# Who issues the expert weights: from ScalarE's queue to SyncE's, at fixed steps

## The reference, cut to what matters

```python
x = x + ss2d(group_norm(x))        # conv 3x3, then a scan over 2304 tokens with 16 states per channel
t = t + linear_attention(ln(t))
t = t + moe(ln(t))                 # the part that the change is about

def moe(x, Wg, W1, W2, W3, b3):    # 8 experts, F = 384, two experts a token
    top_logits, top_idx = top_k(x @ Wg, 2)
    C = sum(onehot(top_idx) * softmax(top_logits)[..., None], axis=-2)
    h = einsum('bsd,edf->bsef', x, W1)
    g = einsum('bsd,edf->bsef', x, W3) + b3
    return einsum('bse,bsef,efd->bsd', C, silu(h) * g, W2)
```

## Time and profile before

| | |
|---|---|
| median of 3 runs | 3860.7 us (3859.01 to 3863.91) |
| the profiled execution | 3844.76 us, span 3842.9 us |
| busy: PE, DVE, ACT, POOL | 3126.6, 3057.3, 2347.0, 2822.3 us |
| w_up and w_down issued by ACT | 258 each |
| w_up and w_down issued by SP | 86 each |

### The profile page before, as it was taken

How to read it: one execution, slowest core, us unless ns; L and a number is a source line. 1 busy time by engine, 2 the same in 40 slices (tenths; PEclk the granted TensorE clock), 3 DMA queues, 4 the chain that set the end, 5 groups by cost and what they waited for, 6 DMA issues and landing times.

```text
span 3842.9 us, 68512 instructions
## 1 busy us (share of the span) xinstructions
PE 3126.6 (81%) x17390; PEld 1997.4 (52%) x17390; DVE 3057.3 (80%) x5492; ACT 2347.0 (61%) x5132; POOL 2822.3 (73%) x2969
## 2 busy tenths in 40 slices
PE   5687888778889888898889888898889888777772
PEld 3233344335556555664556555564556555557772
DVE  2698989998898798888898788888898788944541
ACT  3354576456857766666856767576766767566331
POOL 1465667696758887788968888688968889786534
PEclk9788899789989998999989999999999999888996
DMA  3965656465769678786868768785878867875883
GB/s 85 222 148 132 150 130 171 109 164 136 217 175 258 178 189 213 214 226 155 233 181 240 190 180 223 197 247 142 234 187 237 209 169 211 222 205 186 256 261 117
DMA packets 420320, 730.00 MB, mean 190 GB/s; under 512 B 56203, under 2 KB 313814, under 8 KB 417750
## 3 DMA queue, kind: packets, MB, share of 16 engines
q1 hardware_dynamic: 327190, 534.99, 54.7%
q10 hardware_dynamic: 74304, 152.60, 12.9%
q0 software_dynamic: 18432, 37.93, 3.6%
HBM read 596.93 MB, written 100.07 MB: 181 GB/s over the span
## 4 chain that ended last, share of the span: by engine, by line
POOL 25%; issue 24%; PE 21%; DVE 16%; ACT 7%; DMA 3%; SPq 1%; ACTq 1%; POOLq 1%; DVEq 0%; PEldq 0%
POOL prod L731 12%; DVE state L1652 6%; PE ps_conv L934 5%; PE ps_main L1000 4%; DVE ps_x L1639 3%; POOL got L854 3%; POOL rows_in L831 2%; POOL hidden L843 2%; PE ps_y L1014 2%; PE ps_h L1106 2%; PE ps_x L948 1%; DMA dt_rep<-dt_dram 1%; POOL big_k L808 1%; DMA w_up<-in_w_exp 1%; PE ps_g L1149 1%
## 5 line engine op out<-in xcount | busy, mean ns | idle before, releaser
L731 POOL TENSOR_TENSOR prod<-state,c_rep 128x384 f32<-128x384 f32 x1536 | 1532.7, 1007 | 588.8 <-DVE state L1652 570.6
L1652 DVE TENSOR_TENSOR_SCAN state<-dt_rep,carry,ps_x 128x384 f32<-128x384 f32 x1280 | 1285.6, 1004 | 0.0
L1639 DVE TENSOR_TENSOR ps_x<-ps_x,db_rep 128x384 f32<-128x384 f32 x1536 | 853.1, 555 | 243.4 <-PE ps_x L948 227.9
L1265 ACT ACTIVATE dt_rep<-dt_rep,vecs 128x768 f32<-128x768 f32 x768 | 717.6, 935 | 141.2 <-DMA dt_rep<-dt_dram 101.0
L948 PE MATMUL ps_x<-x_stack,copy 96*128 96x384 bf16 x1536 | 533.8, 350 | 314.7 <-DVE state L1652 309.5
L934 PE MATMUL ps_conv<-gx,w_conv 128*128 128x384 f32 x1728 | 688.0, 505 | 7.8 <-DVE parts L1669 4.6
L948 PEld LDWEIGHTS ps_x<-x_stack,copy 96*128 96x128 bf16 x1536 | 153.8, 100 | 687.1 <-DVE state L1652 495.1
L934 PEld LDWEIGHTS ps_conv<-gx,w_conv 128*128 128x128 f32 x1728 | 300.0, 194 | 216.7 <-issue 128.7
L854 POOL DMA_INDIRECT got<-rows_out,row_of x288 | 279.8, 972 | 132.9 <-DMA rows_out<-u_out 73.0
L1014 PE MATMUL ps_y<-prod,fold 128*32 128x384 f32 x3072 | 359.6, 543 | 19.7 <-POOL prod L731 14.0
L831 POOL DMA_INDIRECT rows_in<-big_u,row_of x288 | 289.4, 1005 | 101.8 <-issue 96.2
(11 more groups left out here) (272 smaller groups left out, 5416.7 us busy)
## 6 DMA issues: line engine op xcount, KB each, us to landing
dt_rep<-dt_dram SPq DMA_DIRECT2D x384, 768.0 KB
w_up<-in_w_exp ACTq DMA_DIRECT2D x258, 384.0 KB
w_down<-in_w_exp ACTq DMA_DIRECT2D x258, 193.5 KB
w_up<-in_w_exp SPq DMA_DIRECT2D x86, 384.0 KB
x_stack<-parts SPq DMA_DIRECT2D x576, 48.0 KB
u_in<-rows_in SPq DMA_DIRECT2D x344, 64.5 KB
rows_out<-u_out SPq DMA_DIRECT2D x344, 64.0 KB
dt_dram<-dt SPq DMA_DIRECT2D x192, 96.0 KB
```

The costliest lines, as they stand in the source:

```text
L731: pool.tensor_tensor(prod[:, k % HS, :], state[:, k % HS, :], c_rep[:, c % 2, :], ALU.mult).then_inc(s_prod.sem, 1)
L1265: act.activation(dt_rep[:, g % XS, q:q + 2, :], dt_rep[:, g % XS, q:q + 2, :], ACT.Exp, scale=decay_rate).then_inc(s_decay.sem, 2)
L1639: dve.tensor_tensor(x_n, x_n, db_rep[:, c % 2, :], ALU.mult).then_inc(s_inflow.sem, 1)
L1652: dve.tensor_tensor_scan(state[:, k % HS, :], dt_rep[:, g % XS, q, :], ps_x[k % XB][:, 0:T], init, ALU.mult, ALU.add).then_inc(s_state.sem, 1)
```

## The change

For all eight images SP reads the experts' numbers and issues both transfers; ACT does neither any more. The first three tiles' weights keep their steps. Those of tile u + 3 of the images 0 to 5 are issued by SP at step TILE[u] + 5 (`T_SPW`), after a wait until ACT has read ps_g of tile u. The last two images keep TILE[u] + 2 and their wait, with one `apart()` more between the wait and the load of the number.

```diff
+T_SPW = 5
 ...
             def weights(m, u):
                 e = sp.value_load(expert_of[0:1, parity(m), u:u + 1], min_val=0, max_val=NE - 1)
                 tall = a["w_exp"][bass.ds(e, 1)].rearrange("o p f -> p (o f)")
-                sp.dma_start(w_up[:, u % WA, :], tall[:, 0:2 * F]).then_inc(s_up[u % WA].sem, 16)
-                if u >= WB:
+                if True:
+                    sp.dma_start(w_up[:, u % WA, :], tall[:, 0:2 * F]).then_inc(s_up[u % WA].sem, 16)
+                if late(m) and u >= WB:
                     due(sp, s_low, m - (B - 2), u - WB + 1)
                 sp.dma_start(w_down[:, u % WB, :], tall[:, 2 * F:3 * F + MF]).then_inc(s_down[u % WB].sem, 16)
...
                 for u in range(WA):
-                    if late(m) and t == T_W + 2 * u:
+                    if t == T_W + 2 * u:
                         if u == 0:
                             due(sp, s_sorted, m, 2)
                             apart()
                         weights(m, u)
-                u = tile_of.get(t - 2)
-                if late(m) and u is not None and u + WA < NU:
-                    sp.wait_ge(*full(m, f"g{u}"))
+                u = tile_of.get(t - (2 if late(m) else T_SPW))
+                if u is not None and u + WA < NU:
+                    sp.wait_ge(*(full if late(m) else read)(m, f"g{u}"))
+                    apart()
                     weights(m, u + WA)
...
-            def weights(m, u):
-                e = act.value_load(expert_of[0:1, parity(m), u:u + 1], min_val=0, max_val=NE - 1)
-                tall = a["w_exp"][bass.ds(e, 1)].rearrange("o p f -> p (o f)")
-                act.dma_start(w_up[:, u % WA, :], tall[:, 0:2 * F]).then_inc(s_up[u % WA].sem, 16)
-                act.dma_start(w_down[:, u % WB, :], tall[:, 2 * F:3 * F + MF]).then_inc(s_down[u % WB].sem, 16)
...
-                if u + WA < NU:
-                    weights(m, u + WA)
...
-                for u in range(WA):
-                    if t == T_W + 2 * u and not late(m):
-                        if u == 0:
-                            due(act, s_sorted, m, 2)
-                            act.sem_inc(s_sp.sem, 1)
-                        weights(m, u)
```

## The result

The changed kernel took 3886.1 us (median of 4, 3882.8 to 3891.6) against 3862.1 us for the kernel before (median of 4). The ratio is 1.0066 with a 95% interval of 1.0052 to 1.0080, that is +20 to +31 us. The forecast was 3863 us with a range up to 3886, and no change as the likeliest case. The profiled execution of the changed kernel has a span of 3884.8 us; that of before, 3842.9, was a short one for its kernel, so the two traces differ by more than the medians do.

What follows compares the result with a forecast made beforehand. PE, DVE and POOL, handing each other work step by step, were taken to bound the kernel, with ACT idle 687 us. Terms -6 (ACT) + 6 (late weights) + 1 (late dt_rep) + 1 (tail) = +2 gave 3863 us, range 3845 to 3886.

Steps and rivals of the forecast that it cites:

- Moved past SP's other issues: SP's list at chunk starts: weight blocks push dt_rep issues back about 1.8 and 2.8 us; 1 us, bounds 0 and 18.
- late dt_rep: Term of the sum for dt_rep issued later on SP around a chunk start among an image's dense tiles: +1 us.
- a landing of 5.6 us: Assumed time from a dt_rep transfer's issue to its landing: 2 us to the first packet, then w_up and w_down's pace.
- ACT's relief: ACT's list without number loads and weight issues: shorter waits of DVE and PE for ACT, -6 us, bounds 0 and 12.
- Late w_up: PE's wait for w_up, issued later by SP, in the dense parts: +6 us, bounds 0 and 18.
- a sign of being wrong: PE's w_up waits over 30 us, named as pointing to rival A or C.
- The tail: Last two images: one extra semaphore instruction on SP for each of their 80 tiles, +1 us.
- A: Rival: late weights decide in the dense part, with landings of about 6 us; +15 to +40, about 3885; chance 0.19.
- C: Rival: SP's crowding delays u_in, dt_rep and x_stack around chunk starts; +8 to +18, about 3874; chance 0.10.
- Its sign: Rival C's sign: ACT's waits for the dt_rep DMA ahead of decays much over today's; dt_rep waits over 50 us.
- The shared queue: Weights and dt_rep in SP's one queue instead of two: same total to move, so nothing charged.

Runs made afterwards that it cites:

- e6: Kernel before, with SP issuing only the first three tiles' weights of images 0 to 5, ACT all others as before: 1.0060, +23 us.
- e5: Changed kernel, with ACT again issuing the first three tiles' weights of images 0 to 5: 1.0012, 3861.8 us.
- e3: Kernel before, with the wait and three number loads (no transfer) in SP's list at TILE[u] + 5, images 0 to 5; ACT still issues weights: 0.9994.
- e7: Changed kernel, with SP issuing the first three tiles' weights of images 0 to 5 ten steps earlier, T_SPW still 5: 0.9987, 3853.9 us.
- e8: Changed kernel, with the first three tiles' weights ten steps earlier and T_SPW = 4: 0.9978, 3849.5 us.
- e10: Kernel before, with SP issuing the first three tiles' weights six steps later, at chunk steps 9, 11, 13, behind the x_stack pieces: 1.0005.
- e11: Changed kernel, with the first three tiles' weights ten steps earlier and T_SPW = 3: 0.9955, 3840.3 us.
- e12: Kernel of e8, with three number loads (1.6 us, no transfer) on ACT where its block stood: 0.9988, 3851.7 us.
- e1: Kernel before, with ACT still issuing the weights of tile u + 3, but at step TILE[u] + 5: 1.0009.
- e13: Kernel before, with ACT issuing the first three tiles' weights of images 0 to 5 two steps later, about when SP did in the change: 1.0002.
- e9: Kernel before, with the wait and three number loads (no transfer) on SP at the first three tiles' steps; ACT issues all weights of images 0 to 5: 1.0010.
- e2: Changed kernel, with three number loads (about 1.6 us, no transfer) on ACT after u_out, where its block stood: 1.0092.
- e4: Changed kernel, with T_SPW = 4 instead of 5: 1.0074.
- e14: Changed kernel, with T_SPW = 3 and nothing else: 1.0023, 3865.2 us.

## Why the prediction was wrong

**The failed step is "Moved past SP's other issues".** It costed the later blocks where they meet x_stack pieces at a chunk start, and took 1 us for "late dt_rep". It never placed the first three blocks of an image, because they "keep their steps" in the code. Those steps are 3, 5 and 7 of a chunk, in the burst of twelve x_stack pieces. On ACT the same steps were harmless; moved to SP they stand in the one list and the one queue on which dt_rep goes out. Measured: 1.0060 for them alone (e6), +23 us, and a gain of the change's whole loss but about 5 us when undone (e5). In numbers of the sum: +1 was booked where +23 belonged. The step also rested on a landing of 5.6 us and on a place, in chunk 0, where the decay came 13.6 us after the issue. In chunk 2 of the kernel before, the transfer behind the burst took 8.4 to 12.0 us to land, 10.3 in the mean of six images, and the decay began 0.3 us after that: there was no room to lose. PE's wait of 14.5 us at L1095, which the earlier trace rows has among those that a faster ACT could shorten, is the one that the late decay made longer. (The prediction also counts one chunk start among the dense tiles. By the code there are two, at steps 160 and 192. e3, which has SP's list time at both, cost nothing.)

**Why these blocks and not the other forty.** The transfer to look at is the fifth of a chunk's eight dt_rep, the first behind the burst. At the other five chunk starts of the kernel before, its decay begins 4.3 to 6.1 us (means of six images) after it has landed; in chunk 2 it is 0.3. The table gives this transfer in chunk 2 for all sixteen traces, as means of the images 2 to 7 in us: issue and landing counted from the chunk's first scan, and last the sum of the six chunks.

| the first three tiles' weights | traces | issued | issue to landing | landed | six chunks |
|---|---|---|---|---|---|
| not in the burst | e7, e8, e10, e11, e12 | 12.8 to 13.3 | 6.3 to 6.9 | 19.1 to 20.2 | 388 to 394 |
| in it, from ACT | before, e1, e3, e5, e13 | 12.6 to 13.5 | 10.1 to 11.1 | 23.4 to 24.6 | 399 to 406 |
| the same, and list time on SP | e9 | 17.8 | 7.6 | 25.4 | 406.5 |
| in it, from SP | after, e2, e4, e6, e14 | 17.5 to 18.2 | 9.0 to 9.5 | 26.5 to 27.5 | 415 to 424 |

The later this transfer lands, the longer the chunk. SP's list time makes the issue late, by 4.5 us in e9, but issued so late it also lands faster (7.6 against 10.3 us), so that 1.8 us remain. With the weights in SP's queue as well (e6), the issue is 0.4 us later again and the landing takes 1.4 us longer than in e9. In ratios: of e6's 0.0060 the list time alone gives 0.0010 (e9) and a later moment alone 0.0002 (e13, whose blocks go out within 3 us of the change's). The rest, about 0.0048 or 18 us, appears only when list time and transfers are on SP together. e9 against e6 is list time on SP in both, and the bytes in ACT's queue or in SP's. What e9 lacks is the later moment, and no run joins that to it. So it is argued from these runs, and not shown by one alone, that the bytes ahead in SP's queue add the 1.4 us. Six landings that are 1.8 us later (e6 against e9) make 11 us, and the six chunks differ by 17; this remainder stays open.

**ACT's relief: right in kind, its size not settled.** I took 6 us with bounds 0 and 12. e12 against e8 gives 4, within the intervals, and e2 against the change 10, hardly clear of them. The "<- issue" waits went as said.

**Late w_up: undersized in waits, and its price is open.** I forecast 5 to 25 waits and 5 to 20 us; the changed kernel has 29 waits and 32.3 us, over the 30 that I had named as a sign of being wrong. From T_SPW = 5 to 4 some 25 us of waits go for nothing (e4) and for 4 us (e8). At T_SPW = 3 the time falls further, by 0.0051 (e4 to e14) and 0.0023 (e8 to e11), with 5.9 and 4.4 us of waits left to lose. The whole step from 5 to 3 is worth 0.0043 and 0.0032, 17 and 12 us, more than the 6 that I booked for lateness. In the traces a gain of that size lies in the dense chunks 4, 5 and 0 of six images: 1309.6 to 1295.1 us (e14), 1313.9 to 1297.8 (e11). So that the dense part lost nothing in the change is a balance of two sides. What that step improves, w_up itself, which blocks stand behind which dt_rep or what the stores meet, I did not take apart. It stays open, and with it the 5 us of e5.

**The tail.** I booked 1 us for it. From the last scan to the end the trace of before has 443.0 us and that of the change 451.4. The nine traces of kernels made from the changed one have 449.9 to 456.9, six of the seven others 443.0 to 448.5 (e9 has 452.6). That is about 5 us in the mean, and no run tested what makes it.

**The rivals.** A (+15 to +40 by late w_up) gave the right side and about the right size by the wrong mechanism: its place, the dense part, was 1.0 us longer in six images, and undoing the first blocks alone takes most of the loss away. C named the mechanism, dt_rep late by SP's crowding at a chunk start, with +8 to +18 and only 0.10, and for the wrong blocks. Its sign, ACT's dt_rep waits over 50 us, was just missed by the change (48.9), and e8 shows 40 us of such waits in a kernel faster than before. So that sign was poor. Better ones are the lengths of the chunks 2 and PE's wait for ACT ahead of the first tile: 35.0 to 36.7 us in the five traces of the table's last line, 14.5 to 18.6 in those of the second, and 9.4 or 9.5 in those of the first.

**The shared queue.** I charged nothing, since the bytes are the same. The runs here: the same first weights at the same moment, from ACT 1.0002, from SP 1.0060, of which list time explains 0.0010. My "nothing" overlooked that the order within the queue can matter where the total doesn't, and that from ACT's queue too the weights were in dt_rep's way: in the burst it took 10.3 us to land before and 6.4 in e10. The sentence of the Trainium skill (DMA: Bandwidth & Descriptors, "Issuing engines are not separate DMA queues") that several issuing engines save only sequencer time agrees as far as the total pace goes, 205 and 202 GB/s in the window of the earlier trace rows; but as a forecast of this change's time it would have led to the same "nothing" as mine. By the section "Queues, rings and completion order" of that page of the Trainium skill each DMA engine takes a queue's descriptors in ring order. That fits the dt_rep behind the weights, which took 9.0 us to land in the change against 7.6 in e9, issued as late.

## What to carry to other kernels

A step that "keeps its place" in the code has moved if its engine has changed: lay every issue of a moved block, the prologue's too, into the new engine's list, and look first where that list is already busy without a gap. Then ask how long before its use the transfer behind that place lands today; where it is 0.3 us, any delay counts. Bulk loads that can be early should not stand ahead of such a transfer in the same queue; here ten steps earlier turned +0.66% into -0.13%, and two steps less for the later ones into -0.45%. Look for a loss in how long equal pieces of the inner loop take, and not only in sums of waits: waits for w_up fell by 25 us with little or no time behind them, and e8, faster than before, has 17 us more of waits for dt_rep. The pieces don't tell all either, as e10 shows, with shorter chunks and the same time.

## What was not expected of the hardware

The 768 KB dt_rep transfer behind the burst took 6.3 to 6.9 us from issue to landing with no weights in the burst, 10.1 to 11.1 with three pairs of them from ACT's queue, and 9.0 to 9.5 with the pairs ahead of it in its own queue, where it was issued some 5 us later. So in this kernel a shorter time from issue to landing went with a later landing. SP's issue of four x_stack pieces took 3.57 us in the change, and of six of them 3.69 us in the kernel before. Loading a number and issuing nothing, 1.6 us forty times an image, was free on SP (0.9994); on ACT the ratio rose by 0.0010 and 0.0026, the first within the intervals.
